# Attention kernel on one core: half of the row tiles take their maximum over 1,024 keys in one VectorE instruction

## The reference

```
xn    = layernorm(x)
q,k,v = xn @ wq + bq, xn @ wk + bk, xn @ wv + bv      # 32 query heads, 8 key/value heads of 16
q,k   = rope(q), rope(k)
s     = softmax(q k^T / 4) v                            # each key head serves 4 query heads
z     = xn W^T + b ;  m = sum_e p_e (xn A_e) B_e
g     = silu(z + min(0.5 |z| / (|m| + 1e-6), 1) * m)
out   = x + s * g
```

## Time and profile before

| | |
|---|---|
| median of three runs | 461.4 us (460.72 to 463.13) |
| the profiled execution, time | 464.08 us |
| the profiled execution, span | 462.3 us |
| mean granted TensorE clock | 0.978 |
| busy in the span: TensorE, VectorE, ScalarE, GpSimd | 97%, 82%, 65%, 19% |

### The profile page before, as it was taken

The page is one execution under the profiler, slowest core; times in us unless marked ns, Lnnn a source line. Parts: engine busy times, 40 slices in busy tenths (PEclk is TensorE's granted clock), DMA queues, the critical chain, the costliest instruction groups (busy, mean ns, idle before and its releaser), DMA issues.

```text
span 462.3 us, 8804 instructions
## 1 busy us (share of the span) xinstructions
PE 449.7 (97%) x3237; PEld 203.6 (44%) x3237; DVE 379.2 (82%) x639; ACT 302.3 (65%) x593; POOL 87.9 (19%) x159
## 2 busy tenths in 40 slices
PE   8898999999999999999999999999999999999995
PEld 3465343443444444444444444444444444433342
DVE  5553588888999999999999999999999999534422
ACT  2120001224888888888888888888888888745594
POOL 8463212434101000000100010010001001014442
PEclk9989599999899999999999999999999999999998
DMA  8979944444000000000000000000000000020011
GB/s 261 319 108 125 114 68 68 68 72 69 2 1 3 1 4 1 1 4 1 3 0 3 3 2 3 1 3 0 3 4 1 3 0 3 2 81 2 20 47 36
DMA packets 13364, 17.45 MB, mean 38 GB/s; under 512 B 3088, under 2 KB 7440, under 8 KB 13328
## 3 DMA queue, kind: packets, MB, share of 16 engines
q1 hardware_dynamic: 11808, 15.84, 18.3%
q10 hardware_dynamic: 1520, 1.12, 0.9%
HBM read 6.72 MB, written 2.10 MB: 19 GB/s over the span
## 4 chain that ended last, share of the span: by engine, by line
PE 88%; DMA 4%; SPq 3%; DVE 2%; ACT 1%; issue 1%; POOL 0%; DVEq 0%
PE st L947 34%; PE oT L901 29%; PE sm L840 8%; PE st L780 7%; PE sm L920 3%; DMA kA<-arena 2%; PE sm L911 2%; DMA idb_sb<-in_identb 2%; PE oT L780 2%; PE st L816 1%; SPq L281 1%; PE sm L923 1%; DVE negmax L638 1%; SPq L313 1%; SPq L287 1%
## 5 line engine op out<-in xcount | busy, mean ns | idle before, releaser
L570 ACT ACTIVATE arena<-st 128x512 f32<-128x512 f32 x512 | 266.9, 600 | 56.5 <-PE st L947 53.5
L646 DVE TENSOR_REDUCE neghalf<-sm 128x1 f32<-128x512 f32 x448 | 270.7, 683 | 2.3 <-PE sm L840 0.4
L840 PE MATMUL sm<-kA,qA 48*128 48x512 f32 x512 | 187.7, 454 | 2.0 <-DMA kA<-arena 1.9
L947 PE MATMUL st<-qA,kA 50*128 50x512 f32 x512 | 177.9, 442 | 1.0 <-ACT arena L570 0.7
L901 PE MATMUL oT<-arena,vg 128*32 128x256 f32 (+3 forms) x1792 | 147.3, 421 | 0.0
L947 PEld LDWEIGHTS st<-qA,kA 50*128 50x128 f32 x512 | 84.2, 185 | 110.7 <-ACT arena L570 87.2
L840 PEld LDWEIGHTS sm<-kA,qA 48*128 48x128 f32 x512 | 85.9, 186 | 23.0 <-issue 14.0
L901 PEld LDWEIGHTS oT<-arena,vg 128*32 128x32 f32 x1792 | 38.7, 108 | 52.7 <-issue 42.2
L638 DVE TENSOR_REDUCE negmax<-sm 128x1 f32<-128x1024 f32 x32 | 38.1, 1221 | 15.9 <-PE sm L840 15.5
L409 POOL TENSOR_TENSOR maxp<-negmax,consts 128x16 bf16<-128x16 f32 x16 | 3.4, 214 | 214.2 <-DVE negmax L653 214.2
L497 ACT ACTIVATE arena<-arena 128x512 fp32r<-128x512 f32 x10 | 6.3, 630 | 57.7 <-POOL arena L369 57.7
(11 more groups left out here) (90 smaller groups left out, 259.6 us busy)
## 6 DMA issues: line engine op xcount, KB each, us to landing
qA<-arena SPq DMA_DIRECT2D x48, 128.0 KB, 5.1
x_sb<-in_x SPq DMA_DIRECT2D x8, 256.0 KB, 5.7
kA<-arena SPq DMA_DIRECT2D x12, 128.0 KB, 6.8
wT_sb<-in_wT SPq DMA_DIRECT2D x1, 1024.0 KB, 9.1
out<-x_sb SPq DMA_DIRECT2D x1, 896.0 KB, 4.0
out<-x_sb SPq DMA_DIRECT2D x4, 224.0 KB, 2.0
z_sb<-in_wq SPq DMA_DIRECT2D x1, 768.0 KB, 10.6
wkv<-in_wk ACTq DMA_DIRECT2D x1, 256.0 KB, 4.1
```

The costliest lines, as they stand in the source:

```text
L570: act.activation(probs[:, s % PB, h, :], st[:, (st_score(0, s, h) - late) % 3, :], ACT.Exp, scale=float(D) ** -0.5).then_inc(st_free, 1)
L646: dve.tensor_reduce(neghalf[:, e // 16, e % 16, j % 2:j % 2 + 1], sm[:, n % 4, :], AX.X, ALU.max, negate=True).then_inc(sm_free, count)
L840: pe.matmul(sm[:, n % 4, :], qA[rows, half, g // 2, h, qt * P:(qt + 1) * P], kA[rows, g // 2, kh * HALF:(kh + 1) * HALF], start=True, stop ...
L947: pe.matmul(st[:, n % 3, :], kA[rows, g // 2, kt * P:(kt + 1) * P], qA[rows, half, g // 2, h, :], start=True, stop=True).then_inc(st_full, 1)
```

## The change

The row tiles e = 0 to 5 and 22 to 31 (`TOGETHER`: j = 0 to 11 and 44 to 63) have both halves in neighbouring banks in every group, since `sm_base(g) + j` is even for an even j below 12, and from 44 on the two extra banks keep it so. For these `whole_row_max` takes one maximum over 1,024 keys straight into `negmax` and frees both banks. The other 16 tiles (j = 12 to 43) stay with `row_max`, and `both_halves` joins those alone (`SINGLES`). TensorE's program is the same. In the first group the extra count for the unused bank of the heads becomes a wait and a semaphore increment of its own.

```diff
+TOGETHER = [e for e in range(32) if 2 * e < OUT1_AT or 2 * e >= OUT0_AT]
+SINGLES = ((6, 16), (0, 6))
+assert TOGETHER == list(range(0, 6)) + list(range(22, 32))
...
+            def whole_row_max(g, j):
+
+                n, e = sm_score(g, j), j // 2
+                dve.wait_ge(sm_full, n + 2)
+                dve.wait_ge(max_parts, 2 * g + e // 16 + 1)
+                dve.tensor_reduce(negmax[:, e // 16, e % 16:e % 16 + 1],
+                                  sm[:, n % 4:n % 4 + 2, :].rearrange("p a n -> p (a n)"), AX.X, ALU.max,
+                                  negate=True).then_inc(sm_free, 2)
+
             def both_halves(g, half):
 
+                first, end = SINGLES[half]
                 dve.wait_ge(sm_free, sm_score(g, 32 * half + 31) + 1)
                 dve.wait_ge(max_parts, 2 * g + half + 1)
-                dve.tensor_tensor(negmax[:, half, :], neghalf[:, half, :, 0], neghalf[:, half, :, 1],
-                                  ALU.min).then_inc(max_both, 1)
+                dve.tensor_tensor(negmax[:, half, first:end], neghalf[:, half, first:end, 0],
+                                  neghalf[:, half, first:end, 1], ALU.min).then_inc(max_both, 1)
...
-                    row_max(g, j, 2 if first and j == OUT1_AT - 1 else 1)
+                    if j // 2 not in TOGETHER:
+                        row_max(g, j, 1)
+                    elif j % 2 == 0:
+                        whole_row_max(g, j)
+                    if first and j == OUT1_AT - 1:
+                        dve.wait_ge(sm_free, sm_score(g, j) + 1)
+                        dve.sem_inc(sm_free, 1)
```

## The result

The changed kernel takes 476.5 us (median of 4, 475.9 to 477.1) where the one before, in the same measurement, takes 461.1 us (460.3 to 463.1): a ratio of 1.0327 with a 95% interval of 1.0289 to 1.0366, or 15.5 us more. The forecast was 476.4 us.

A forecast was written before the change was run, and what follows sets the result against it. VectorE was taken as the bound between about 114 and 397 us. Six passages at 12.6 us, a tail of 1.0 and a head of 1.4 gave +15.0 us on 461.4: 476.4 us, range 468 to 484.

The forecast's parts named there:

- one loop: Straddling row on TensorE and VectorE: row end, bank freed, value block, bank full; 3.09 or 2.88 us against 2.28.
- Saved: VectorE's merged maxima: 0.056 us per row, 0.90 us per group, 6.3 us over seven groups.
- Added waits: Merged rows on VectorE also wait for GpSimd to have read the earlier maxima; counted as nothing, 0.08 us a row for the range.
- Stalls: VectorE waits at five rows per group whose two scores have a value block between them; 3.15 us per passage.
- Per passage: From j = 44 to 63 and the next 0 to 11: 3.15 us stall minus 0.90 saved, 2.1 us after small idling.
- the 0.12 that the forecast let them absorb: Trace passage on VectorE, 20.28 us, against its start-to-start sum, 20.16; the difference was taken as idling that absorbs added stall.
- Head and tail: First group's j = 0 to 11: 1.4 us, between 0 and 2.6; seventh group's j = 44 to 63: 1.0 us.
- Singles: Unmerged maxima, j = 12 to 43: they keep their pace, nothing carries over and nothing is won back.
- Range: Total time 468 to 484 us; lower from blocks costing 1.00 and no head, upper from lost overlap and a 2.6 us head.
- the block inside a row: Value block between a row's two scores on TensorE, five rows per group; claimed stalls of 0.17 to 1.06 us there.
- some 5% in hand: TensorE in the steady stretch: ahead by the whole ring of four banks, waiting for VectorE about once per burst.
- faster: Rival for the whole kernel: VectorE alone decides, 6.3 us are saved, 455 us; chance 0.07.

The follow-up runs named there:

- the first experiment: The same sixteen row tiles merged as in the change, but without the added wait for GpSimd's reading, against the kernel before: 477.5 us, ratio 1.0333.
- the two runs that merged the least harmful rows: Against the kernel before, merged were only the first row of each burst (464.3 us, ratio 1.0050), or only rows that looked free (462.9 us, ratio 1.0037).

## Why the prediction was right

The direction, the size and the place came out of one loop, and nearly all of its terms held. **Saved:** merged rows start 1.14 us apart as forecast, so 0.056 us each. The estimate of 125 ns per row that follows from the Trainium skill ("VectorE: DVE Perf Modes", section on the TRN2 errata) is not borne out by this trace either. **Added waits:** nothing, shown by the first experiment. **Stalls:** forecast 0.17, 0.81, 0.60, 0.51 and 1.06 us at j = 46, 52, 58, 2 and 8, measured 0.09, 0.82, 0.61, 0.39 and 1.08; 3.15 against 3.0 in sum. **Per passage:** VectorE goes from j = 44 to 44 of the next group in 42.54 us, 2.08 more than before, forecast 2.1. That it fits so closely is partly luck: the stalls were 0.15 smaller, and the 0.12 that the forecast let them absorb was not idle time to begin with, since the closing minimum starts only when the last maximum has ended (237.20 against 237.17), in the change too (241.74 against 241.70). **Head and tail:** from the first maximum to that of j = 12 the head takes 10.7 us in place of 9.6, 1.1 more (forecast 1.4), the part behind the last j = 44, up to the end of the span, 1.1 us (1.0). **Singles:** they keep their pace. **Range:** its lower bound takes off 4.4 us where its own terms (0.67 in six passages, 0.21 in the tail) give 4.2; this changes nothing.

The span of the profiled execution is 475.3 us, 2.0 under the 477.3 that the sum gave it. The first 112 us were 1.8 us shorter in it, before any changed instruction runs; that is one execution against another and not the change. The medians differ by 15.5.

The mechanism is the one that the forecast named, two banks that come free together and a start that needs both, and each costs by itself: 4.5 us and 4.8 us with no instruction merged. What the forecast put too simply is the weight of the block inside a row. It said that a row whose scores share a burst loses nothing. That held in the change, but the eleven such rows merged alone cost 5 us, and the five others alone 4 and not 18. The block says where the stall shows once all sixteen rows are merged; that it is needed for a stall is not so. Shown are each half of the mechanism by itself and that the wide instruction is not dear. That both together feed each other I argue from the loop and from 2.08 us per group against 0.6 and 0.6; no run shows it apart from the merging.

Wrong in the prediction was that TensorE has some 5% in hand: where it counts, it has nothing. It had named VectorE as the bound for time that is added to it; the expectations behind it took this to hold for time that is taken away too, and it does not: in the two runs that merged the least harmful rows VectorE's saving was gone at once. The kernel before shows why, at j = 3 and 12 on TensorE and at the heads before j = 12 (timelines of TensorE and of VectorE):

```profile
237.76 0.50 PE L840 MATMUL sm<-kA,qA 48*128 48x512 f32 x1
...
243.85 0.66 PE L911 MATMUL sm<-id_sb,wkv 128*128 128x128 f32 x4
...
244.44 0.49 PE L840 MATMUL sm<-kA,qA 48*128 48x512 f32 x1
```

```profile
244.54 0.26 DVE L695 RECIPROCAL rsum<-sm 128x16 f32<-128x16 f32 x1
```

TensorE takes 244.44 - 237.76 = 6.68 us from j = 3 to j = 12 with its two blocks of 512 columns, and at most 0.2 of it is a wait for VectorE (at j = 5, which starts at 238.63 behind the maximum of j = 1). VectorE takes 9 x 0.598 + 0.93 = 6.3. There TensorE, which in part waits for ScalarE's ring, is the slower one, and only the four banks that it had filled ahead kept VectorE busy. The scaling of the heads starts at 244.54, right behind the transposes (244.51) and as the last maximum ends; with half-wide blocks, at the full clock, it starts 0.08 us before that maximum ends. Two scalings a group make nearly all of the 0.18 us. So "faster" was further off than its 0.07 said: even without stalls, 6.3 us would hardly have come in. How much TensorE alone would take was not measured.

## What to carry to other kernels

A ring of buffers that two tight engines share is worth more than the fixed cost of an instruction: merging two reads makes four single buffers into two double ones, and the reader starts later and releases later. Before merging, write down the loop from one release to the next, with everything that stands in the writer's queue in between, and compare it with the time of two merged reads; here 3.1 us against 2.3. And an engine that is 99% busy may only just be fed: check with a small saving first whether savings on it come in at all.

## What the runs showed of the hardware

The overlap of VectorE's neighbouring maxima survives a wait instruction between them, where what it waits for is there: 1.14 us apart for records of 1.21. TensorE's granted clock can fall when work is taken from it: 0.98 in the mean before, but with half of the value products gone it was 0.50 for stretches of 40 us, and a kernel with less work took 540 us in place of 477.
